# Graph transformer layer: the down projection of the steady slots alternates two graphs and two PSUM banks matmul by matmul

## Chip, cores and metric

One core of one Trainium2 chip. The metric is the device time of one launch in microseconds (us); the median of the runs is compared.

## What is computed

128 graphs of 128 nodes with 384 features go through one transformer layer with a dense bias, and then an outer residual and a layer norm:

```python
scores = einsum(q, k) * dh ** -0.5 + adj[:, None]        # 8 heads of 48
x1 = rmsnorm(x + softmax(scores) @ v @ wo + bo) * alpha1 + gamma1
ff = silu(x1 @ w1 + b1) @ w2 + b2                        # 384 -> 1536 -> 384
y  = rmsnorm(x1 + ff) * alpha2 + gamma2
out = layernorm(x + y)
```

Everything is fp32. Each weight product is made of three passes, since every operand is held as a rounded high part and the rest (`PASSES`: low by high, high by low, high by high).

## The kernel before, in words

All weights stay on chip. The graphs are taken in 64 groups of two (`PAIR`; the two graphs of a group are b=0 and b=1). The program of every engine is a list of 68 slots written out by hand (`run_slots`). In slot t five groups are in work at once, each in another stage: the projections to q, k and v of group t-1 (`g_proj`), attention of t-2 (`g_attn`), the up projection of t-3 (`g_ff1`), the down projection and the last norms of t-4 (`g_ff2`), and the transposition of the input of group t. Slots 4 to 64 run the steady program; slots 2 and 3 (`starting`) and 65 to 67 (`ending`) have orders of their own.

Each engine works through its own list strictly in order, and the engines meet at semaphores only. The orders in a steady slot are:

- TensorE (`@block.tensor`, lines 658 to 687): `scores` of both graphs, `down` b=0 (36 matmuls into the bank `ps_rows0`), `down` b=1 (36 into `ps_rows1`), `project_qk` (54 matmuls in three groups of 18; the third waits for `qk_ready[0]`, line 539), `transpose_probs`, `transpose_x1`, `project_v` b=0, `context` of both, `project_v` b=1 (which waits for `x1T_lo[0]`, line 551), `output_product` of both (each waits for `ctx_lo[b]`, line 491), `transpose_x`, and `up` (108 matmuls).
- VectorE (`@block.vector`, lines 1034 to 1079): `bias_and_max` twice, `normalise` 0, `residual2` 0, `normalise` 1, `norm2_and_stats` 0, `residual2` 1, `layer_norm` 0, `norm2_and_stats` 1, `layer_norm` 1, `keys_out`, the low parts of x1 transposed (`transposed_lo`, which makes `x1T_lo`), `values_out` 0, `context_lo` 0 and 1, `values_out` 1, and so on.
- ScalarE (lines 816 to 847): 16 exponentials, `sum_of_squares` 0 of the second residual (waits for `res2_ready[0]`), a load of the Silu table, `sum_of_squares` 1, `queries_out` 0 and 1.
- GpSimd (lines 413 to 438): the inverse roots of b=0 (RMS, then standard deviation), those of b=1, and after them one addition of 128x768 elements, x1 plus b2 (line 433), which waits only for the transposition of x1.
- SyncE issues the loads, the store of y (it waits for both `layer_norm`s) and after it the ten moves of q and k (line 383).

`residual2` adds x1 to the result in `ps_rows[b]` (line 955), `norm2_and_stats` scales by the inverse RMS (line 960), adds the outer residual (966) and takes the statistics (968, 970), and `layer_norm` is one `tensor_scalar` (line 974). `keys_out` (line 901) empties the third group of `project_qk`.

Of the kernel before, what the change touches and what calls it, by code (L numbers as in the profile page):

```python
# [35 lines left out]
P = 128  # L36
PAIR = 2
# [5 lines left out]
PASSES = ((LO, HI), (HI, LO), (HI, HI))  # L43
# [7 lines left out]
def build_layer(nc, x, adj, wq, bq, wk, bk, wv, bv, wo, bo, w1, b1, w2, b2,  # L51
                alpha1, gamma1, alpha2, gamma2, out):
    graphs, nodes, d = x.shape
# [7 lines left out]
    fc = f // P  # L61
# [6 lines left out]
    with ctx:  # L68
# [221 lines left out]
        def live(g):  # L290

            return 0 <= g < groups

        def through(g, each=1):

            return (g + 1) * each
# [146 lines left out]
        def _(pe):  # L443
# [59 lines left out]
            def down(g, b):  # L503

                last_attn = g + LAG_FF2 - LAG_ATTN - 1
                if live(last_attn):
                    pe.wait_ge(res1_ready[b], through(last_attn))
                elif live(g - 1):
                    pe.wait_ge(res2_ready[b], through(g - 1))
                if b == 0 and live(g + LAG_FF2 - 1):  # L510
                    pe.wait_ge(xT_lo[1], through(g + LAG_FF2 - 1))
                if b == 1:
                    pe.wait_ge(x1T_lo[1], through(g + 1 if ending(g + LAG_FF2) and live(g + 1) else g))
                for m in range(fc):
                    if b == 0 and m % 2 == 0:
                        pe.wait_ge(h_lo[m // 2], through(g))
                    for i, (sta, mov) in enumerate(PASSES):
                        mm = pe.matmul(ps_rows[b][:, 0:d], h[:, sta, m, b * P:(b + 1) * P], w2_s[:, mov, m, :],  # L518
                                       start=(m == 0 and i == 0), stop=(m == fc - 1 and i == len(PASSES) - 1))
                mm.then_inc(down_done[b], 1)  # L520

            def project_qk(g):
                for i in range(2):
                    pe.wait_ge(xT_lo[i], through(g))
                for n, blocks in enumerate((((wq_s, 0), (wq_s, 1)), ((wq_s, 2), (wk_s, 0)),
                                            ((wk_s, 1), (wk_s, 2)))):
                    if g == 0 and n < 2:
                        pe.wait_ge(weight_split, (n + 1) * kd)

                    if n == 0 and live(g - LAG_FF1 + LAG_PROJ - 1):  # L530
                        pe.wait_ge(silu_ready[fc // 2 - 2], through(g - LAG_FF1 + LAG_PROJ - 1))
                    elif n == 0 and live(g - 1):
                        pe.wait_ge(v_ready[1], through(g - 1))
                    elif n == 1 and live(g - LAG_FF1 + LAG_PROJ - 1):
                        pe.wait_ge(silu_ready[fc // 2 - 1], through(g - LAG_FF1 + LAG_PROJ - 1))
                    elif n == 1 and live(g):
                        pe.wait_ge(xT_lo[0], through(g))
                    elif n == 2:
                        pe.wait_ge(qk_ready[0], through(g))
                    for j, (w, c) in enumerate(blocks):  # L540
                        mm = passes(ps_work[n % 2][:, j * toks:(j + 1) * toks], [
                            (lambda part, kb=kb: w[:, part, kb, c * P:(c + 1) * P],
                             lambda part, kb=kb: xT[:, part, kb, :]) for kb in range(kd)])
                    mm.then_inc(qk_done[n], 1)
# [69 lines left out]
            def slot_program(t, parity):  # L614
                g_proj, g_attn, g_ff1, g_ff2 = t - LAG_PROJ, t - LAG_ATTN, t - LAG_FF1, t - LAG_FF2
                if starting(t):
                    for b in range(PAIR):
                        scores(g_attn, b)
                    project_qk(g_proj)
                    for b in range(PAIR):  # L620
                        project_v(g_proj, b)
                    for b in range(PAIR):
                        transpose_probs(g_attn, b)
                    for b in range(PAIR):
                        context(g_attn, b)
                    if live(g_ff1):
                        transpose_x1(g_ff1, parity)
                    if t == LAG_ATTN:
                        pe.wait_ge(weight_split, out_units)
                    for b in range(PAIR):  # L630
                        output_product(g_attn, b)
                    for i in range(2):
                        transpose_x(t, i)
                    if live(g_ff1):
                        pe.wait_ge(weight_split, up_units)
                        up(g_ff1)
                    return
                if ending(t):
                    if live(g_attn):
                        for b in range(PAIR):  # L640
                            scores(g_attn, b)
                    down(g_ff2, 0)
                    if live(g_ff1):
                        transpose_x1(g_ff1, parity)
                    if live(g_attn):
                        transpose_probs(g_attn, 0)
                    down(g_ff2, 1)
                    if live(g_attn):
                        transpose_probs(g_attn, 1)
                    if live(g_ff1):  # L650
                        up(g_ff1)
                    if live(g_attn):
                        for b in range(PAIR):
                            context(g_attn, b)
                        for b in range(PAIR):
                            output_product(g_attn, b)
                    return
                if live(g_attn):
                    for b in range(PAIR):
                        scores(g_attn, b)  # L660
                if live(g_ff2):
                    if t == LAG_FF2:
                        pe.wait_ge(weight_split, len(units))
                    for b in range(PAIR):
                        down(g_ff2, b)
                if live(g_proj):
                    project_qk(g_proj)
                if live(g_attn):
                    for b in range(PAIR):
                        transpose_probs(g_attn, b)  # L670
                if live(g_ff1):
                    transpose_x1(g_ff1, parity)
                if live(g_proj):
                    project_v(g_proj, 0)
                if live(g_attn):
                    for b in range(PAIR):
                        context(g_attn, b)
                if live(g_proj):
                    project_v(g_proj, 1)
                if live(g_attn):  # L680
                    for b in range(PAIR):
                        output_product(g_attn, b)
                if live(t):
                    for i in range(2):
                        transpose_x(t, i)
                if live(g_ff1):
                    up(g_ff1)
# [164 lines left out]
        def _(dve):  # L852
# [26 lines left out]
            def normalise(g, b):  # L879
                for half in range(2):  # L880
                    heads = slice(half * hp, (half + 1) * hp)
                    dve.wait_ge(exp_ready[b], through(g, 2) - 1 + half)
                    dve.reciprocal(row_inv[:, b, heads], row_sum[:, b, heads]).then_inc(inv_ready[b], 1)
                    dve.wait_ge(inv_ready[b], through(g, 2) - 1 + half)
                    dve.tensor_tensor(probs[:, b, heads], probs[:, b, heads],  # L885
                                      row_inv[:, b, heads].unsqueeze(2).to_broadcast([P, hp, P]),
                                      ALU.mult).then_inc(probs_ready[b], 1)
# [89 lines left out]
            def slot_program(t, parity):  # L977
# [56 lines left out]
                if live(g_attn):  # L1034
                    for b in range(PAIR):
                        bias_and_max(g_attn, b, parity)
                    normalise(g_attn, 0)
                if live(g_ff2):
                    residual2(g_ff2, 0, parity)
                if live(g_attn):  # L1040
                    normalise(g_attn, 1)
                if live(g_ff2):
                    norm2_and_stats(g_ff2, 0)
                    residual2(g_ff2, 1, parity)
                    layer_norm(g_ff2, 0)
                    norm2_and_stats(g_ff2, 1)
                    layer_norm(g_ff2, 1)
                if live(g_proj):
                    keys_out(g_proj)
                if live(g_ff1):  # L1050
                    transposed_lo(g_ff1, 0, ps_work[0], x1T_hi, x1T, x1T_lo)
                    transposed_lo(g_ff1, 1, ps_rows[1], x1T_hi, x1T, x1T_lo)
# [53 lines left out]
```

## Time and profile before

| | us |
|---|---|
| median of 3 runs (2967.24 to 2967.73) | 2967.57 |
| the profiled execution | 2968.35 |
| its span in the profile | 2966.6 |
| TensorE busy | 2923.2 (99%) |
| VectorE busy | 1974.3 (67%) |
| ScalarE busy | 1441.6 (49%) |
| GpSimd busy | 697.8 (24%) |

The profile has one row for each group of instructions: its start and its length in us, engine, line, operation, output and inputs, and how many. Where an engine had been idle, the end of the row says for how long and who ended the wait. PE is the matmuls of TensorE and PEld its weight loads, DVE is VectorE, ACT is ScalarE, POOL is GpSimd, and SPq is the queue of SyncE. A steady slot lasts 45.43 us and looks the same every time, so one is read for all.

### The profile page before, as it was taken

Reading aid. Unit: us, or ns where it says so; the run is one execution under the profiler, and the core shown is the slowest. Engines: PE = TensorE matmul, PEld = TensorE weight load, DVE = VectorE, ACT = ScalarE, POOL = GpSimd, SP = SyncE. Lnnn points to the kernel's source line nnn. Section 1 sums busy time; section 2 is a strip of 40 time slices with the busy share of each in tenths; the row PEclk is TensorE's granted clock in tenths of the full one; section 3 lists DMA queues with packets and bytes.
Section 4 is the critical chain, followed back from the end, with each engine's and each line's share of the span. In section 5 each row is a group of like instructions: output and inputs, shape, how many; then the busy total and the mean of one; then the engine's idle time right before and its main releaser. Section 6 shows DMA issues by size and latency. Waiting matters only on the chain.

```text
span 2966.6 us, 62752 instructions
## 1 busy us (share of the span) xinstructions
PE 2923.2 (99%) x25216; PEld 2871.9 (97%) x25216; DVE 1974.3 (67%) x3621; ACT 1441.6 (49%) x4260; POOL 697.8 (24%) x968
## 2 busy tenths in 40 slices
PE   7999999999999999999999999999999999999998
PEld 6999999999999999999999999999999999999998
DVE  5766666666666676666666666666666667666665
ACT  5455455454554454544545545545445445454442
POOL 0222222222222222222222222222222222222222
PEclk9999999999999999999999999999999999999999
DMA  5211211211212112112122121121121211211200
GB/s 163 74 57 47 69 53 50 69 47 56 68 35 69 56 47 69 52 52 69 41 63 59 45 68 54 50 69 48 55 69 36 68 56 47 69 52 51 63 28 28
DMA packets 155491, 171.93 MB, mean 58 GB/s; under 512 B 18624, under 2 KB 155200, under 8 KB 155200
## 3 DMA queue, kind: packets, MB, share of 16 engines
q1 hardware_dynamic: 155200, 167.91, 19.1%
q8 instruction: 200, 3.28, 0.5%
q14 instruction: 91, 0.75, 0.1%
HBM read 92.35 MB, written 25.17 MB: 40 GB/s over the span
## 4 chain that ended last, share of the span: by engine, by line
PE 96%; DVE 1%; ACT 1%; SPq 1%; issue 0%; POOL 0%; DMA 0%; POOLq 0%; ACTq 0%; DVEq 0%
PE ps_work L450 48%; PE ps_rows L518 27%; PE ps_rows L450 6%; PE ps_att L462 4%; PE ps_att L471 4%; PE ps_att L482 2%; PE ps_att L486 2%; PE ps_work L560 2%; PE ps_rows L560 1%; SPq L331 0%; ACT probs L704 0%; DVE w_s L864 0%; SPq L383 0%; ACT squares L719 0%; DVE neg_max L876 0%
## 5 line engine op out<-in xcount | busy, mean ns | idle before, releaser
L450 PE MATMUL ps_work<-x1T,w_s 128*128 128x256 f32 x6912 | 847.7, 283 | 2.9 <-ACT h_raw L760 2.2
L450 PEld LDWEIGHTS ps_work<-x1T,w_s 128*128 128x128 f32 x6912 | 835.6, 188 | 3.5 <-ACT h_raw L760 2.4
L518 PE MATMUL ps_rows<-w_s,h 128*128 128x384 f32 x4608 | 822.2, 339 | 10.7 <-DVE x1T L922 7.0
L518 PEld LDWEIGHTS ps_rows<-w_s,h 128*128 128x128 f32 x4608 | 801.4, 189 | 18.7 <-issue 7.4
L760 ACT ACTIVATE h_raw<-ps_work,b_col 128x256 f32<-128x256 f32 x768 | 322.7, 471 | 478.5 <-PE ps_work L450 471.3
L704 ACT ACTIVATE probs<-probs,neg_max 128x128 f32<-128x128 f32 x1024 | 396.0, 388 | 238.5 <-DVE neg_max L876 238.5
L946 DVE TENSOR_TENSOR h<-h_raw,h 128x512 fp32r<-128x512 f32 x384 | 359.3, 936 | 13.2
L944 DVE CAST h<-h_raw 128x512 fp32r<-128x512 f32 x384 | 165.7, 431 | 302.7 <-ACT h_raw L760 302.2
L419 POOL TENSOR_TENSOR x_last<-x_last,rows 128x768 f32<-128x768 f32 x64 | 117.7, 1839 | 773.8 <-PE ps_att L462 773.8
L407 POOL TENSOR_SCALAR mean_sq<-sum_sq 128x1 f32<-128x1 f32 x256 | 69.0, 270 | 975.4 <-ACT squares L719 975.3
L450 PE MATMUL ps_work<-wv_s,xT 128*128 128x384 f32 x1152 | 235.2, 348 | 2.1 <-ACT qk_flat L740 1.2
L450 PE MATMUL ps_work<-xT,wq_s 128*128 128x256 f32 x1728 | 217.4, 283 | 4.0 <-DVE wq_s L864 2.9
L450 PEld LDWEIGHTS ps_work<-xT,wq_s 128*128 128x128 f32 x1728 | 214.9, 191 | 4.7 <-issue 3.5
L450 PE MATMUL ps_work<-xT,wk_s 128*128 128x256 f32 x1728 | 213.5, 280 | 0.0
L450 PE MATMUL ps_rows<-wo_s,ctxT 128*128 128x384 f32 x1152 | 210.7, 336 | 1.3 <-DVE ctxT L891 1.2
L450 PEld LDWEIGHTS ps_work<-wv_s,xT 128*128 128x128 f32 x1152 | 196.4, 188 | 14.9 <-issue 12.1
L450 PEld LDWEIGHTS ps_work<-xT,wk_s 128*128 128x128 f32 x1728 | 207.5, 188 | 0.3 <-ACT qk_flat L737 0.3
L450 PEld LDWEIGHTS ps_rows<-wo_s,ctxT 128*128 128x128 f32 x1152 | 200.3, 188 | 2.1 <-issue 1.1
L719 ACT ACTIVATE squares<-x 128x384 f32<-128x384 f32 x128 | 67.5, 527 | 272.8 <-DVE x L929 272.6
L704 ACT ACTIVATION_READ_ACCUMULATOR probs<-probs,neg_max 128x1 f32 x1024 | 192.1, 188 | 0.0
L723 ACT ACTIVATE probs<-ps_att 128x1024 f32<-128x1024 f32 x128 | 124.5, 1024 | 131.9 <-PE ps_att L471 131.9
L885 DVE TENSOR_TENSOR probs<-probs,row_inv 128x512 f32<-128x512 f32 x256 | 178.3, 697 | 8.8
(86 smaller groups left out, 3440.7 us busy)
## 6 DMA issues: line engine op xcount, KB each, us to landing
qk<-qk_flat SPq DMA_DIRECT2D x384, 96.0 KB, 2.4
x_in<-in_x SPq DMA_DIRECT2D x64, 384.0 KB, 3.2
x_res<-in_x SPq DMA_DIRECT2D x64, 384.0 KB, 3.9
x_last<-in_x SPq DMA_DIRECT2D x64, 384.0 KB, 3.2
out<-y SPq DMA_DIRECT2D x63, 384.0 KB, 2.5
bias<-in_adj SPq DMA_DIRECT2D x64, 128.0 KB, 3.8
qk<-qk_flat SPq DMA_DIRECT2D x128, 64.0 KB, 2.1
qk<-qk_flat SPq DMA_DIRECT2D x128, 32.0 KB, 2.0
```

Source lines behind the costliest of these rows:

```text
L419: pool.tensor_tensor(x_last[:], x_last[:], row(GAMMA2), ALU.add).then_inc(x_last_biased, 1)
L450: mm = pe.matmul(ps_out, stationary(sta), moving(mov), start=(i == 0), stop=(i == n - 1))
L462: mm = pe.matmul(ps_att[b][:, at:at + P], qk[p0:p0 + dh, Q, c, b * P:(b + 1) * P], qk[p0:p0 + dh, K, c, b * P:(b + 1) * P], start=True, st ...
L471: mm = pe.transpose(ps_att[b][:, head * P:(head + 1) * P], probs[:, b, head, :], ident[:])
L518: mm = pe.matmul(ps_rows[b][:, 0:d], h[:, sta, m, b * P:(b + 1) * P], w2_s[:, mov, m, :], start=(m == 0 and i == 0), stop=(m == fc - 1 and ...
L560: mm = pe.transpose(ps_out[:, at:at + P], rows_in[:, b, kb * P:(kb + 1) * P], ident[:])
L704: e = act.activation(probs[:, b, head, :], probs[:, b, head, :], ACT.Exp, bias=neg_max[:, b, head:head + 1], accum_out=row_sum[:, b, head: ...
L723: act.activation(probs[:, b].rearrange("p h n -> p (h n)"), ps_att[b][:], ACT.Copy).then_inc(probsT_ready[b], 1)
L760: e = act.activation(h_raw[:, m % 2, j * toks:(j + 1) * toks], ps_work[m % 2][:, j * toks:(j + 1) * toks], ACT.Silu, bias=b1_col[:, 2 * m ...
L885: dve.tensor_tensor(probs[:, b, heads], probs[:, b, heads], row_inv[:, b, heads].unsqueeze(2).to_broadcast([P, hp, P]), ALU.mult).then_inc ...
L944: dve.tensor_copy(hi, h_raw[:, m % 2, :]).then_inc(h_hi[m], 1)
L946: dve.tensor_tensor(h[:, LO, 2 * m:2 * m + 2, :].rearrange("p c n -> p (c n)"), h_raw[:, m % 2, :], hi.bitcast(F32), ALU.subtract).then_in ...
```

## The change

A new function `down_alternating` takes the place of the two calls of `down` in the steady slots. It runs the same 72 matmuls, but each pass of each block is done for b=0 and then for b=1, so that successive matmuls go to different banks, and both sums are finished at the end. All its waits stand ahead of or inside the joint loop. On VectorE the steady order is changed too: `normalise` 0 and 1, `residual2` 0 and 1, `norm2_and_stats` 0, `layer_norm` 0, then `keys_out`, and only then `norm2_and_stats` 1 and `layer_norm` 1. ScalarE, GpSimd and SyncE keep their programs, and so do the starting and ending slots.

```diff
--- before.py
+++ after.py
@@ -518,6 +518,27 @@
                         mm = pe.matmul(ps_rows[b][:, 0:d], h[:, sta, m, b * P:(b + 1) * P], w2_s[:, mov, m, :],
                                        start=(m == 0 and i == 0), stop=(m == fc - 1 and i == len(PASSES) - 1))
                 mm.then_inc(down_done[b], 1)
+
+            def down_alternating(g):
+
+                last_attn = g + LAG_FF2 - LAG_ATTN - 1
+                for b in range(PAIR):
+                    if live(last_attn):
+                        pe.wait_ge(res1_ready[b], through(last_attn))
+                    elif live(g - 1):
+                        pe.wait_ge(res2_ready[b], through(g - 1))
+                if live(g + LAG_FF2 - 1):
+                    pe.wait_ge(xT_lo[1], through(g + LAG_FF2 - 1))
+                pe.wait_ge(x1T_lo[1], through(g))
+                for m in range(fc):
+                    if m % 2 == 0:
+                        pe.wait_ge(h_lo[m // 2], through(g))
+                    for i, (sta, mov) in enumerate(PASSES):
+                        for b in range(PAIR):
+                            mm = pe.matmul(ps_rows[b][:, 0:d], h[:, sta, m, b * P:(b + 1) * P], w2_s[:, mov, m, :],
+                                           start=(m == 0 and i == 0), stop=(m == fc - 1 and i == len(PASSES) - 1))
+                            if m == fc - 1 and i == len(PASSES) - 1:
+                                mm.then_inc(down_done[b], 1)
 
             def project_qk(g):
                 for i in range(2):
@@ -661,8 +682,7 @@
                 if live(g_ff2):
                     if t == LAG_FF2:
                         pe.wait_ge(weight_split, len(units))
-                    for b in range(PAIR):
-                        down(g_ff2, b)
+                    down_alternating(g_ff2)
                 if live(g_proj):
                     project_qk(g_proj)
                 if live(g_attn):
@@ -1034,19 +1054,18 @@
                 if live(g_attn):
                     for b in range(PAIR):
                         bias_and_max(g_attn, b, parity)
-                    normalise(g_attn, 0)
+                    for b in range(PAIR):
+                        normalise(g_attn, b)
                 if live(g_ff2):
-                    residual2(g_ff2, 0, parity)
-                if live(g_attn):
-                    normalise(g_attn, 1)
+                    for b in range(PAIR):
+                        residual2(g_ff2, b, parity)
+                    norm2_and_stats(g_ff2, 0)
+                    layer_norm(g_ff2, 0)
+                if live(g_proj):
+                    keys_out(g_proj)
                 if live(g_ff2):
-                    norm2_and_stats(g_ff2, 0)
-                    residual2(g_ff2, 1, parity)
-                    layer_norm(g_ff2, 0)
                     norm2_and_stats(g_ff2, 1)
                     layer_norm(g_ff2, 1)
-                if live(g_proj):
-                    keys_out(g_proj)
                 if live(g_ff1):
                     transposed_lo(g_ff1, 0, ps_work[0], x1T_hi, x1T, x1T_lo)
                     transposed_lo(g_ff1, 1, ps_rows[1], x1T_hi, x1T, x1T_lo)
```

## Rows read from the trace of the kernel before

**Rows 1.** The page's first part: busy time and instructions by engine.

```profile
PE 2923.2 (99%) x25216; PEld 2871.9 (97%) x25216; DVE 1974.3 (67%) x3621; ACT 1441.6 (49%) x4260; POOL 697.8 (24%) x968
```

**Rows 2.** Chain of work, one steady slot: start, length, what.

```profile
1508.08 12.68 PE ps_rows L518 x72
1520.76 6.34 PE ps_work L450 x54
...
1534.76 3.12 PE ps_rows L450 x18
```

**Rows 3.** Chain of work, the ending slots.

```profile
2913.37 6.25 PE ps_rows L518 x36
...
2946.12 12.51 PE ps_rows L518 x72
```

**Rows 4.** Instructions in order of time, one steady slot, from down to keys_out.

```profile
1518.28 0.51 ACT L719 ACTIVATE squares<-y 128x384 f32<-128x384 f32 x1
...
1518.90 1.28 ACT L822 ACT_TABLE_LOAD   x1
...
1521.97 0.53 DVE L955 TENSOR_TENSOR y<-ps_rows,x 128x384 f32<-128x384 f32 x1
...
1522.53 0.53 ACT L719 ACTIVATE squares<-y 128x384 f32<-128x384 f32 x1 [2.35 <-DVE y L955]
...
1523.05 0.82 ACT L737 ACTIVATE qk_flat<-ps_work,bq_col 128x256 f32<-128x256 f32 x2
...
1523.66 3.24 PEld L450 LDWEIGHTS ps_work<-xT,wk_s 128*128 128x128 f32 x27
...
1524.20 0.62 DVE L960 SCALAR_TENSOR_TENSOR y<-y,inv_rms,rows 128x384 f32<-128x384 f32 x1 [0.72 <-POOL inv_rms L410]
...
1527.17 0.48 DVE L974 TENSOR_SCALAR y<-y,mean_var,inv_std 128x384 f32<-128x384 f32 x1 [0.95 <-POOL inv_std L410]
1527.57 0.87 DVE L901 TENSOR_SCALAR qk_flat<-ps_work,bk_col 128x256 f32<-128x256 f32 x2
```

**Rows 5.** The same view and slot, from the moves of q and k on.

```profile
1528.54 7.06 SPq L383 DMA_DIRECT2D qk<-qk_flat  x10
...
1529.65 1.85 POOL L433 TENSOR_TENSOR x<-x,rows 128x768 f32<-128x768 f32 x1 [2.51 <-PE ps_rows L560]
...
1530.48 0.69 DVE L922 TENSOR_TENSOR x1T<-ps_work,x1T 128x512 fp32r<-128x512 f32 x1 [2.04 <-ACT x1T L747]
...
1531.08 0.41 DVE L922 TENSOR_TENSOR x1T<-ps_rows,x1T 128x256 fp32r<-128x256 f32 x1
...
1532.24 0.42 DVE L911 TENSOR_TENSOR v_first<-ps_work,rows 128x256 f32<-128x256 f32 x1 [0.74 <-PE ps_att L486]
...
1532.85 0.55 DVE L891 TENSOR_TENSOR ctxT<-ps_att,ctxT 128x384 fp32r<-128x384 f32 x1
1532.91 1.53 PEld L450 LDWEIGHTS ps_work<-wv_s,xT 128*128 128x128 f32 x9 [0.20 <-issue]
...
1534.43 3.13 PEld L450 LDWEIGHTS ps_rows<-wo_s,ctxT 128*128 128x128 f32 x18
```

**Rows 6.** The same view, ending slots.

```profile
2898.14 0.55 POOL L410 TENSOR_TENSOR inv_std<-var_eps,neg_half 128x1 f32<-128x1 f32 x1
2898.66 1.84 POOL L433 TENSOR_TENSOR x<-x,rows 128x768 f32<-128x768 f32 x1
2898.73 1.99 DVE L974 TENSOR_SCALAR y<-y,mean_var,inv_std 128x384 f32<-128x384 f32 x1 [0.95 <-POOL inv_std L410]
...
2922.08 0.41 DVE L922 TENSOR_TENSOR x1T<-ps_rows,x1T 128x256 fp32r<-128x256 f32 x1
...
2922.61 7.76 PEld L518 LDWEIGHTS ps_rows<-w_s,h 128*128 128x128 f32 x36 [2.58 <-issue]
```

**Rows 7.** Busy time by stretch: stretch, length, engines, granted clock, DMA share, GB/s.

```profile
2922.60:2930.50 7.90, 7.86 (x36) 7.89 (x37) 2.20 (x5) 0.00 (x0) 0.74 (x2) 0.78 0.00 0
```

## Prediction, made before the changed kernel was run

> **What bounds the kernel.** I read the busy times first, then the chain of work through one steady slot, then the instructions of that slot in order of time. TensorE is busy for 99% of the span [rows 1], and in a steady slot the chain is TensorE alone, piece behind piece, such as 12.68 us of down projection, 6.34 of q and k, 3.12 of output product [rows 2]. So a change can help only by making matmuls themselves shorter, and it hurts as soon as one of TensorE's waits ends late. The edit touches 61 slots (t = 4 to 64); 1 us in each would be 61 us.
>
> **The matmuls.** Nothing is removed or added: 72 matmuls and 72 weight loads of the same shapes in each slot. New is that 71 successive pairs change the bank, where one did. The trace has no continuous alternation; it has single changes. The 36 matmuls into one bank take 6.25 us, 173.6 ns each; 72 with one change take 12.51 [rows 3], so a change costs 0 to 0.02 us by rounding. The output product is 18 matmuls of the same width with one change in 3.12 us [rows 2], 173.3 ns each, against 18 x 173.6 = 3.125, so a change costs -12 to +3 ns. Both together leave 0 to 3 ns; over 70 x 61 = 4270 further changes that is 0 to 13 us. I take 0, since the stretch with one change in 18 is no slower per matmul than that with none. TensorE's waits move too: those of b=1 on `res1_ready[1]` and `x1T_lo[1]` go from the middle to the start. Both were signalled in the slot before (the low parts of x1 end at 1531.49 for a down that starts 22 us later [rows 2, 5]), so they cost nothing, and `h_lo` is needed later than before, not earlier.
>
> **The moved end of b=0.** Before, b=0 is done halfway, at about 1514.4, and its second norm is computed while b=1 runs. Now b=0 ends one matmul ahead of b=1, at 1520.76 - 0.17 = 1520.59 on the clock of the slot shown [rows 2]. Everything behind it must fit into the gaps up to TensorE's next waits. I go through them with the durations of [rows 4]; a waiting engine starts 0.03 to 0.04 us after the one it waits for.
>
> ScalarE: residual2 of b=0 runs from 1520.63 to 1521.16. The Square starts at 1521.20, the table load 0.62 later (as 1518.28 to 1518.90) and lasts 1.28, to 1523.10; that load was hidden in the down projection and now stands behind it. The Square of b=1 starts there, and the query copy 0.52 later (as 1522.53 to 1523.05), at 1523.62, and lasts 0.82, to 1524.44. TensorE's third group of q and k needs that bank at the tenth of the 27 loads, 1523.66 + 9 x 0.117 = 1524.71 [rows 4]. It fits, with some 0.2 us left. Cost 0; if the cover is missed by 0.1 us, 6 us in all.
>
> VectorE up to `keys_out`: norm 2 of b=0 starts at most 1.67 us behind its Square (1522.53 to 1524.20), so by 1522.87, and layer_norm 0 follows 2.97 later (1524.20 to 1527.17), 1525.84 to 1526.32. Then `keys_out` waits for the last matmul of q and k, 1520.76 + 6.34 = 1527.10 [rows 2], and runs from 1527.14 to 1528.01; before, it began at 1527.57 [rows 4]. That is 0.43 us earlier, and nobody on the chain gains by it.
>
> VectorE behind `keys_out`: what queues behind that wait is norm 2 of b=1, whose inputs are there by then (GpSimd has its inverse RMS by 1525.8 + 1.67 = 1527.5 at the latest). It starts at 1527.93, since a ready instruction starts some 0.08 before its predecessor's end (1530.48 + 0.69 against 1531.08 [rows 5]). layer_norm 1 is due 2.97 later, at 1530.90, where it was done at 1527.65 [rows 4]: 3.7 us later.
>
> Here it meets GpSimd. The addition of 128x768 elements (line 433) stands in GpSimd's list behind the inverse deviation of b=1. In before it starts at 1529.65, when x1 is transposed [rows 5], and layer_norm 1 is long over. Now it is released by the same event as layer_norm 1. The ending slots hold just this case: the inverse deviation ends at 2898.69, GpSimd's addition starts at 2898.66, layer_norm at 2898.73, and the latter takes 1.99 us and not 0.48; it ends 0.22 behind the addition [rows 4, 6]. So layer_norm 1 waits for the addition. In the new slot: addition 1530.83 to 1532.68, layer_norm 1 until 1532.90.
>
> The Trainium skill (SBUF - State Buffer, Who interferes with whom) has this as an exclusive lock: whichever of VectorE and GpSimd issues first keeps the shared port pair, and the other blocks for the whole instruction; `tensor_scalar` is named among those that can take it. The trace agrees, with 1.99 us against 0.48. By the rule alone the sum would be the same.
>
> What is late next: the low part of x1 (0.69) starts at 1532.81 and ends at 1533.50 instead of 1531.17. `project_v` of b=1 waits for it and started its weights at 1532.91 [rows 5]. From such a low part to the weight load behind it there are 0.12 us (2922.49 to 2922.61 [rows 6]), so it starts at 1533.62. **Stall: 0.71 us.** Then `ctx_lo[0]`: from the first low part to the end of line 891 VectorE needs 0.60 (to 1531.08), 0.33 for the second part, 0.61 (1532.24 to 1532.85) and 0.55 [rows 5], which gives 1534.90, seen by TensorE at 1535.02; the output product is now due at 1534.43 + 0.71 = 1535.14. It fits by 0.1. From there the slot runs as before.
>
> Side effects off the chain: SyncE waits for layer_norm 1, so the ten moves of q and k start near 1533.8 and not 1528.54; with 7.06 us of issue [rows 5] they end at 1541, and `scores` needs them ten us later. The next loads start 2 us later and have more room than that.
>
> **Sum.** 61 x 0.71 = 43 us, with 0 for the matmuls. The profiled execution took 2968.35 (span 2966.6 and 1.75 around it), so 3011.3 by its measure; the median is 0.78 lower, so 3010.6. The stall is a difference of chained starts and may be off by 0.2 us; 0.5 to 0.9 us gives 31 to 55. With up to 13 for the bank changes, 2998 to 3036, and the larger ends of all are unlikely together.
>
> **Rivals.**
> - *layer_norm 1 is not held* (chance 0.13): it gets in ahead of GpSimd, or the addition starts later than I think. Then it ends at 1531.38, the low part at 1531.98, seen at 1532.10, ahead of 1532.91, and no wait of TensorE ends late: 2967.6, no change. It decides at 0.07 us, the lead of the addition over layer_norm in [rows 6]; that the same queue order gave that lead there speaks against it.
> - *Alternation makes matmuls shorter* (0.04): 384 columns at 2.4 GHz are 160 ns of the 173.6. If all of the rest went, 4392 x 13.6 = 60 us would come back against 43 lost, and the time would be 2951. It decides at 9.8 ns a matmul; the stretch with one change in 18 shows 0.3.
> - *ScalarE is late as well* (0.08): the query copy misses 1524.71 by up to 0.3 us, everything behind shifts with it, and up to 18 us come on top: 3012 to 3029.
> - *TensorE's clock falls* (0.02): each slot now has nearly a microsecond without a matmul. In the ending slots the mean granted clock was 0.78 in a stretch [rows 7] behind 2.58 us of idling, so in part at the lower level of 1.2 GHz. Its 36 weight loads took 7.76 us [rows 6] against 6.25 for 36 matmuls at full clock [rows 3], 1.5 lost; 61 such losses are 92: 3102. The Trainium skill (TensorE: Matmul & The Clock Gate, A second HAM failure mode: psum-queue depth-cycling) warns that cycling through banks makes TensorE pause and its clock swing; by that page this rival would be likelier, but the single changes of bank here show no pause.
> - *Another wait is late too* (0.02), such as the 0.1 us at the output product: above 3032.
>
> **How the numbers follow.** The forecast has 0.71. The range 2990 to 3032 holds it with the ScalarE case, 0.79; outside lie no change, the gain and the two dearer cases. What a measurement can tell from no change is 0.2%, 6 us, or 0.1 us of stall in a slot. Slower: 0.71 + 0.08 + 0.02 + 0.02 = 0.83; same 0.13; faster 0.04.
>
> **What would show it.** Right: a layer_norm of about 2 us in every steady slot beside line 433, the steady slot 46.1 us long, and TensorE's idling ahead of `project_v`'s second half put down to x1T, some 0.7 us 61 times. The 72 matmuls of down stay at 12.7 us. Wrong: layer_norm at 0.48 us, a down piece shorter or longer than 12.7, idling ahead of the q and k product, or a granted clock under 1 in the middle of the span.

## The result and the profile after

The changed kernel takes 3012.07 us (median of 4 runs, 3009.1 to 3013.83) against 2967.65 before: a ratio of 1.0148, 95% interval 1.0135 to 1.0162. It is 44.4 us slower; 3010.6 was forecast, in a range of 2990 to 3032. The span of the profiled execution is 3007.3 us, 40.7 more than before, and that execution (3009.1) is the fastest of the four.

TensorE's waits, longest first (who waited for whom: us in total, times, longest), have one line that the kernel before has nothing to answer to:

```profile
PE ps_work L450 <- DVE x1T L942: 39.4, 61, 0.6
```

It is the second `project_v`, 61 times, once in each changed slot. The chain of work (start, length, what) through one slot shows where that wait comes from:

```profile
1528.66 12.68 PE ps_rows L538 x72
1541.34 6.36 PE ps_work L450 x54
...
1547.72 0.88 DVE qk_flat L921 x2
1548.60 0.54 DVE y L980
...
1550.89 0.56 POOL inv_std L410
...
1551.47 1.30 DVE y L994
...
1553.38 0.69 DVE x1T L942
...
1554.20 1.83 PE ps_work L450 x9
1556.03 3.12 PE ps_rows L450 x18
...
1574.78 12.68 PE ps_rows L538 x72
```

The down projection is as long as in [rows 2], 12.68 us; the next one starts 46.12 us after this one, where a slot took 45.43. Between the q and k product and `project_v` the chain leaves TensorE: `keys_out` (L921), the norm of b=1 (L980 to L990), GpSimd's inverse deviation (L410), layer_norm (L994), the low part of x1 (L942). In before this stretch was TensorE alone. (layer_norm's length is split here, 1.30 us and then 0.60 in which the chain finds nothing that it waits for; the rows below have it whole.) The same slot in order of time, in the lines that answer to [rows 4, 5]:

```profile
1541.30 1.02 DVE L975 TENSOR_TENSOR y<-ps_rows,x 128x384 f32<-128x384 f32 x2 [1.41 <-PE ps_rows L538]
1541.89 0.53 ACT L739 ACTIVATE squares<-y 128x384 f32<-128x384 f32 x1 [2.94 <-DVE y L975]
...
1542.53 1.28 ACT L842 ACT_TABLE_LOAD   x1
...
1544.24 3.24 PEld L450 LDWEIGHTS ps_work<-xT,wk_s 128*128 128x128 f32 x27
...
1544.35 0.82 ACT L757 ACTIVATE qk_flat<-ps_work,bq_col 128x256 f32<-128x256 f32 x2
...
1547.72 0.88 DVE L921 TENSOR_SCALAR qk_flat<-ps_work,bk_col 128x256 f32<-128x256 f32 x2 [0.82 <-PE ps_work L450]
1548.51 0.61 DVE L980 SCALAR_TENSOR_TENSOR y<-y,inv_rms,rows 128x384 f32<-128x384 f32 x1
...
1551.41 1.83 POOL L433 TENSOR_TENSOR x<-x,rows 128x768 f32<-128x768 f32 x1
1551.47 1.98 DVE L994 TENSOR_SCALAR y<-y,mean_var,inv_std 128x384 f32<-128x384 f32 x1 [0.95 <-POOL inv_std L410]
...
1553.38 0.68 DVE L942 TENSOR_TENSOR x1T<-ps_work,x1T 128x512 fp32r<-128x512 f32 x1
...
1554.17 1.53 PEld L450 LDWEIGHTS ps_work<-wv_s,xT 128*128 128x128 f32 x9 [0.89 <-issue]
...
1554.90 1.01 DVE L911 TENSOR_TENSOR ctxT<-ps_att,ctxT 128x384 fp32r<-128x384 f32 x2
1555.70 2.44 PEld L450 LDWEIGHTS ps_rows<-wo_s,ctxT 128*128 128x128 f32 x14
```

The two lines to look at are those at 1551.41 and 1551.47: GpSimd's addition of line 433 starts 0.06 us ahead of layer_norm 1, and layer_norm takes 1.98 us instead of 0.48. It does so in all 61 changed slots (1.98 to 1.99 us). The profile gives GpSimd's times only roughly, so the lead of 0.06 us is less certain than the length on VectorE. The low part of x1 (L942), the weight loads of `project_v` and what follows stand in its train.

### The profile page after: what moved, and what is told of

It is laid out like the page before. It is cut to its first block, busy times and chain, and to the rows that moved or that the text cites. A ratio compares the mean times of both kernels' runs of the same rounds, so it can differ in the third digit from the quotient of the medians.

```text
span 3007.3 us, 62752 instructions
## 1 busy us (share of the span) xinstructions
PE 2924.2 (97%) x25216; PEld 2870.6 (95%) x25216; DVE 2055.4 (68%) x3621; ACT 1448.1 (48%) x4260; POOL 675.1 (22%) x968
## 4 chain that ended last, share of the span: by engine, by line
PE 83%; DVE 11%; issue 2%; POOL 2%; ACT 1%; SPq 1%; DMA 0%; POOLq 0%; ACTq 0%; DVEq 0%
PE ps_work L450 44%; PE ps_rows L538 26%; PE ps_rows L450 6%; PE ps_att L462 4%; DVE y L994 3%; DVE qk_flat L921 2%; DVE x1T L942 1%; DVE stats L988 1%; DVE y L986 1%; PE ps_rows L518 1%; POOL inv_std L410 1%; DVE y L980 1%; PE ps_work L581 1%; SPq L331 0%; PE ps_rows L581 0%
## 5 line engine op out<-in xcount | busy, mean ns | idle before, releaser
L538 PE MATMUL ps_rows<-w_s,h 128*128 128x384 f32 x4392 | 779.3, 338 | 3.7 <-DVE w_s L884 3.7
L538 PEld LDWEIGHTS ps_rows<-w_s,h 128*128 128x128 f32 x4392 | 759.7, 188 | 11.2 <-DVE w_s L884 3.9
L407 POOL TENSOR_SCALAR mean_sq<-sum_sq 128x1 f32<-128x1 f32 x256 | 49.7, 194 | 1122.8 <-ACT squares L739 1117.4
L450 PE MATMUL ps_work<-wv_s,xT 128*128 128x384 f32 x1152 | 233.8, 347 | 41.5 <-DVE x1T L942 39.4
L994 DVE TENSOR_SCALAR y<-y,mean_var,inv_std 128x384 f32<-128x384 f32 x128 | 156.2, 1220 | 121.0 <-POOL inv_std L410 121.0
```

What stands on the lines that cost most here:

```text
L450: mm = pe.matmul(ps_out, stationary(sta), moving(mov), start=(i == 0), stop=(i == n - 1))
L994: dve.tensor_scalar(y[:, b, :], y[:, b, :], mean_var[:, b, 0:1], inv_std[:, b:b + 1], ALU.subtract, ALU.mult).then_inc(y_ready[b], 1)
```

## The experiments

The theory: the time is lost where VectorE's order puts layer_norm 1 behind `keys_out`, into GpSimd's addition, with the low part of x1 queued behind it; the alternation itself costs the matmuls nothing. The rivals: alternation costs (matmuls, or the late end of b=0); the later queue costs, collision or none; line 433 and layer_norm slow each other whoever is first. The kernel before was run beside each; its median was 2967.6 to 2967.8.

### Moving keys_out alone

The kernel before, `down` b=0 and then b=1, with one edit:

```diff
                     layer_norm(g_ff2, 0)
-                    norm2_and_stats(g_ff2, 1)
-                    layer_norm(g_ff2, 1)
                 if live(g_proj):
                     keys_out(g_proj)
+                if live(g_ff2):
+                    norm2_and_stats(g_ff2, 1)
+                    layer_norm(g_ff2, 1)
```

> The kernel before with one thing moved: on VectorE keys_out stands ahead of norm2_and_stats 1 and layer_norm 1; TensorE does not alternate. Theory of the held layer_norm: layer_norm 1 starts 2.97 us behind a keys_out that ends at the same place of the slot as in the changed kernel, meets line 433 and takes 1.98 us, project_v of b=1 waits for x1T, slot 46.12 us, time 3007 to 3014. Rival, that the alternation or the late end of b=0 costs the time: about 2968.

Measured: 3011.65 us, ratio 1.0149 (1.0133 to 1.0164). TensorE's waits have the same line as in the changed kernel:

```profile
PE ps_work L450 <- DVE x1T L922: 39.4, 61, 0.6
```

So this one move makes the whole loss, without alternation.

### VectorE's new order without the alternation

The kernel before with VectorE's part of the diff, TensorE's part left out.

> The kernel before with VectorE's whole new order and TensorE's old one (b=0, then b=1). Theory (the loss sits in VectorE's order, whatever TensorE does): layer_norm 1 is held behind keys_out, x1T comes 0.65 us late, slot 46.12 us, 3007 to 3014, the same as the changed kernel, though b=0 is done 6 us earlier and the table load is hidden again. Rival, that alternation and its late b=0 carry part of the 44 us: less than 3000.

Measured: 3010.24 us, ratio 1.0143 (1.0129 to 1.0157), and 39.4 us of the same wait in 61 times. Alternating or not, the time is the same once VectorE's order is the new one.

### The alternation without VectorE's new order

The changed kernel with VectorE's part of the diff left out.

> The changed kernel with VectorE's old order: TensorE alternates, residual2 0 stands ahead of normalise 1 and residual2 1 behind norm2_and_stats 0. Theory (the alternation is free for the matmuls, the late end of b=0 is dear for the queues): the down piece stays 12.68 us; residual2 1 comes at about 4.2 us behind the end of down, ScalarE's queries_out behind its Square is 2.1 us late for the third group of q and k, and keys_out behind layer_norm 1 holds the transposes of x1 for 0.8 us more; slot 48.3 us, time 3130 to 3160. Rival, that only VectorE's new order costs time: 2968.

Measured: 3190.03 us, ratio 1.075 (1.0732 to 1.0768): more than expected. The waits of TensorE are the two foreseen:

```profile
PE ps_work L450 <- ACT qk_flat L757: 137.0, 61, 2.2
PE ps_work L581 <- DVE qk_flat L921: 18.7, 35, 0.5
```

The first is 2.25 us a slot, where 2.1 was expected. In order of time, and then the busy time of two stretches (in the last columns: granted clock, DMA share, GB/s):

```profile
1540.06 0.52 ACT L739 ACTIVATE squares<-y 128x384 f32<-128x384 f32 x1 [2.62 <-DVE y L975]
...
1540.58 1.19 ACT L757 ACTIVATE qk_flat<-ps_work,bq_col 128x256 f32<-128x256 f32 x3
...
1541.45 3.55 PE L450 MATMUL ps_work<-xT,wk_s 128*128 128x256 f32 x18 [2.25 <-ACT qk_flat L757]
```

```profile
1541.45:1545.00 3.55, 3.55 (x19) 3.55 (x20) 2.22 (x5) 0.68 (x2) 0.98 (x3) 0.62 0.28 58
...
1570.00:1600.00 30.00, 27.21 (x254) 26.23 (x253) 18.94 (x34) 15.54 (x49) 9.49 (x11) 1.00 0.14 40
```

The 18 matmuls behind the wait take 3.55 us instead of 2.12 (a third of 6.34 [rows 2]), at a mean granted clock of 0.62: part of them ran at 1.2 GHz. The next stretch holds another such stall (TensorE is busy for 27.21 of its 30 us) and kept its clock, so the clock falls behind some stalls and not behind others. What a fall costs a slot is read from the chain of work, from one down piece to the next (71 of its 72 matmuls are on the chain here):

```profile
1522.29 12.52 PE ps_rows L538 x71
...
1571.81 12.52 PE ps_rows L538 x71
...
1620.49 12.52 PE ps_rows L538 x71
```

The slot with the fallen clock lasts 49.52 us, the one without 48.68. The matmuls lose twice as much as these 0.84 us: in the chain the 18 take 1.43 us more, and the 16 transposes of the probabilities behind them 2.14 us instead of 1.75. But TensorE then comes late to the transposes of x1 and doesn't have to wait for `keys_out`; that wait is there 35 times and not 61. In the whole trace, the first changed slot left aside, 25 slots of 59 have such a fall, and together they are 21 us longer than they would be at the 48.66 us of the slots without one.

The expected slot of 48.3 us gives 2967.8 + 61 x 2.9 = 3145 us, so the expectation misses some 45 us, and less than half of that is the clock. About as much, some 21 us, is the plain slot: it is not 48.3 us, with 0.15 us more in the first stall, and the first four transposes behind the second one take 0.63 us where they take 0.44 without a wait. The rest lies in the first changed slot and in the ending ones.

### keys_out back behind layer_norm 1

The changed kernel with `keys_out` in its old place relative to the norm of b=1, `normalise` and `residual2` in the new one.

> The changed kernel with keys_out back behind layer_norm 1. Theory: with both sums of down ready only at its end, layer_norm 1 starts 9.0 us behind that end and is not held (line 433 waits for transposes that wait for keys_out), 0.48 us; keys_out ends near 10.2 us behind the end of down, where the transposes of x1 were due at 7.8: a stall of 2.5 us, slot 47.9 us, 3120 or, if the clock falls behind such stalls as it did with TensorE alone alternating, up to 3170. Rival, that the place of keys_out is what costs the 44 us in the changed kernel: 2968.

Measured: 3130.15 us, ratio 1.0555 (1.054 to 1.057). In order of time:

```profile
1516.47 0.48 DVE L994 TENSOR_SCALAR y<-y,mean_var,inv_std 128x384 f32<-128x384 f32 x1 [0.95 <-POOL inv_std L410]
1516.86 0.87 DVE L921 TENSOR_SCALAR qk_flat<-ps_work,bk_col 128x256 f32<-128x256 f32 x2
...
1517.85 0.42 PEld L581 LDWEIGHTS ps_work<-ident,x 128*128 128x128 f32 x4 [2.52 <-issue]
```

layer_norm 1 is not held, but the transposes of x1 (L581) wait for `keys_out`: TensorE's loads had been idle for 2.52 us. So with the late b=0 the old place of `keys_out` is dearer than the new one: 163 us against 44. The slot is 47.92 us, as expected, where the clock holds. In the profiled execution, the slowest of the four (3141.14 us), it fell in 12 slots of 59, each about 1.5 us longer, 19 us together; its mean was 0.988.

### The addition in halves

The changed kernel with GpSimd's long instruction cut in two:

```diff
-                    pool.tensor_tensor(x1[:, 1 - parity], x1[:, 1 - parity], row(B2),
-                                       ALU.add).then_inc(x1_b2_ready, 1)
+                    for b in range(PAIR):
+                        e = pool.tensor_tensor(x1[:, 1 - parity, b, :], x1[:, 1 - parity, b, :],
+                                               rows[:, B2, :], ALU.add)
+                        e.then_inc(x1_b2_ready, 1)
```

> The changed kernel with GpSimd's addition of line 433 split in two of 128x384, one for each graph. Theory of the held layer_norm: the first half holds it for some 0.95 us instead of 1.83, layer_norm 1 takes about 1.1 us, x1T_lo comes 0.15 us ahead of project_v, the slot is 45.43 to 45.5 us, time 2968 to 2973. Rival, that the later place of the norm in VectorE's queue costs it by itself: 3010 as before.

Measured: 2968.28 us, ratio 1.0001 (0.9992 to 1.0011).

```profile
1531.27 2.10 POOL L434 TENSOR_TENSOR x<-x,rows 128x384 f32<-128x384 f32 x2
1531.34 1.16 DVE L996 TENSOR_SCALAR y<-y,mean_var,inv_std 128x384 f32<-128x384 f32 x1 [0.95 <-POOL inv_std L410]
```

layer_norm got in between the two halves, 1.16 us, and the x1T wait is gone from the list. The queue is as late as in the changed kernel up to layer_norm's start; only the hold is shorter.

### The addition moved away

The changed kernel with line 433 behind the inverse roots of attention.

> The changed kernel with GpSimd's addition of line 433 moved behind the inverse roots of attention, 10 us later in the slot. Theory of the held layer_norm: layer_norm 1 takes 0.48 us in every slot, x1T is ready 0.8 us ahead of project_v, slot 45.43 us, 2966 to 2972; the addition now meets the first split of h, which has over a microsecond of room. Rival, that the queue behind keys_out is late by itself: 3010, or over 2980 where it is late in part.

Measured: 2967.11 us, ratio 1.0 (0.999 to 1.0009).

```profile
1530.23 0.48 DVE L994 TENSOR_SCALAR y<-y,mean_var,inv_std 128x384 f32<-128x384 f32 x1 [0.94 <-POOL inv_std L410]
...
1530.62 0.69 DVE L942 TENSOR_TENSOR x1T<-ps_work,x1T 128x512 fp32r<-128x512 f32 x1
...
1532.24 1.53 PEld L450 LDWEIGHTS ps_work<-wv_s,xT 128*128 128x128 f32 x9 [0.20 <-issue]
...
1539.52 1.84 POOL L437 TENSOR_TENSOR x<-x,rows 128x768 f32<-128x768 f32 x1
...
1540.94 0.71 DVE L964 CAST h<-h_raw 128x512 fp32r<-128x512 f32 x1 [0.86 <-ACT h_raw L780]
```

layer_norm 1 is 0.48 us; x1T is ready at 1531.31, 0.9 us ahead of the loads of `project_v` at 1532.24. The addition now stretches the first cast of h, 0.71 us against 0.43, and nobody waits.

### The addition issued second

The changed kernel with a tiny instruction ahead of the addition:

```diff
+                    pool.tensor_scalar(idle[:], neg_half[:], 1.0, None, ALU.mult)
                     pool.tensor_tensor(x1[:, 1 - parity], x1[:, 1 - parity], row(B2),
```

> The changed kernel with one tiny GpSimd instruction (128x1, some 0.2 us) put ahead of the addition of line 433, so that layer_norm 1 is issued first. Theory (who comes first holds the other for its whole length): layer_norm 1 takes 0.48 us in the steady slots, the addition ends a little later, by 0.2 to 0.5 us, and is in nobody's way; x1T in time, slot 45.43 us, 2966 to 2970. Rival, that the two slow each other down whenever they overlap, whoever is first: layer_norm 1 over 1 us and a slot over 45.6 us, 2980 or more.

Measured: 2966.53 us, ratio 0.9997 (0.9987 to 1.0006).

```profile
1530.09 0.23 POOL L434 TENSOR_SCALAR idle<-neg_half 128x1 f32<-128x1 f32 x1
1530.15 0.48 DVE L996 TENSOR_SCALAR y<-y,mean_var,inv_std 128x384 f32<-128x384 f32 x1 [0.95 <-POOL inv_std L411]
...
1530.27 2.05 POOL L435 TENSOR_TENSOR x<-x,rows 128x768 f32<-128x768 f32 x1
```

layer_norm starts 0.12 us ahead of the addition and takes its plain 0.48; now the addition is the one that is longer, 2.05 against 1.83. One more instruction of 0.23 us wins back the whole loss (45.5 us from 3012.07). A hold shared by both is ruled out.

The edit also adds a tile of 4 bytes a partition (`idle`), and the times of the matmuls differ a little: the down piece takes 12.83 us in the chain and the up projection 12.87 where it was 12.98, and the slot is 45.40 us. Whether the new tile moved the others is not shown. The hold itself is still there in this kernel: the low part of h (L968) takes 2.20 us instead of 0.69 once in every slot, as its counterpart does in the kernel before. So it is the order that freed layer_norm.

### layer_norm 1 behind the low parts of x1

The changed kernel, with VectorE's `layer_norm(g_ff2, 1)` behind the two `transposed_lo` of x1.

> The changed kernel with layer_norm 1 behind the two transposed_lo of x1 on VectorE. Theory of the held layer_norm: it is held as before, about 1.5 us, but nothing that TensorE needs at once is queued behind it; x1T is ready where it was in the kernel before, ctx_lo[0] some 0.3 us ahead of the output product; slot 45.43 us, 2966 to 2972. Rival, that alternation costs the time: 3010. Rival, that everything behind keys_out is late anyway: x1T waits again, over 2990.

Measured: 2967.66 us, ratio 1.0 (0.9991 to 1.0009).

```profile
1530.25 0.69 DVE L942 TENSOR_TENSOR x1T<-ps_work,x1T 128x512 fp32r<-128x512 f32 x1 [0.53 <-ACT x1T L767]
1530.60 1.84 POOL L433 TENSOR_TENSOR x<-x,rows 128x768 f32<-128x768 f32 x1
...
1530.86 0.41 DVE L942 TENSOR_TENSOR x1T<-ps_rows,x1T 128x256 fp32r<-128x256 f32 x1
...
1531.19 1.46 DVE L994 TENSOR_SCALAR y<-y,mean_var,inv_std 128x384 f32<-128x384 f32 x1
...
1532.68 1.53 PEld L450 LDWEIGHTS ps_work<-wv_s,xT 128*128 128x128 f32 x9 [0.20 <-issue]
```

Here layer_norm is held all the same, 1.46 us, and it costs nothing: what TensorE needs next has already run. The hold is a loss only with the low part of x1 behind it.

### The kernel before with the addition in halves

The same split in the kernel before, for the ending slots, where one held layer_norm lies on the chain.

> The kernel before with the addition of line 433 in two halves. In the steady slots nothing collides, so nothing changes; in the two ending slots layer_norm 1 is held for 1 us less, and one of them has it on the chain: 0 to 1.5 us less in all, 2966 to 2968, which the times can hardly tell. Rival, that a split addition slows GpSimd's queue: up to 61 x 0.25 us more if it were on the chain, 2983.

Measured: 2966.82 us, ratio 0.9998 (0.9989 to 1.0007). The held layer_norm of the ending slots is shorter, here in the chain of work:

```profile
2934.24 1.16 DVE y L976
```

It was 1.98 us. But the cast and the low part of h, next on VectorE, took 2.00 and 0.70 us in the chain before and take 1.17 and 2.21 now: the hold has moved to the next instruction, and 0.14 us of the 0.82 are left. No time beyond the measurement's uncertainty came of it, so neither this nor any other run beats the kernel before by more than its interval.

## Why the prediction came out right

The slot shown above is 20.58 us later on its clock than that of [rows 2] (1541.34 against 1520.76 for the end of down), so every time of the forecast can be laid beside it.

- **The matmuls cost nothing more**: 12.68 us for 72 matmuls with 71 changes of bank. The bounds of 0 to 13 us for the changes were worked out from the ending slots, where 72 matmuls take 12.51 us [rows 3]; like against like is the steady piece, 12.68 [rows 2] and 12.68. That the change would be slower by the alternation itself is refuted from both sides: `keys_out` moved alone makes the same loss without it, and the changed kernel with the addition moved away alternates and loses nothing.
- **ScalarE fits, by less than forecast**: the query copy was to run to 1524.44; it ends at 1545.17, that is 1524.59. The Square of b=0 starts at 1541.89, not 1541.78, since residual2 of b=0 started later than 0.04 us behind its matmul. The loads needed the bank at 1544.24 + 9 x 0.117 = 1545.29, so 0.12 us were left, not 0.27. The rival of a late ScalarE was close.
- **VectorE up to keys_out**: forecast 1527.14, measured 1547.72, that is 1527.14.
- **layer_norm 1 held**: addition and layer_norm forecast for 1530.83 and 1530.90, measured 1530.83 and 1530.89; its end forecast for 1532.90, measured 1532.87. Two rows of the ending slots gave this, and with them the length: 1.99 us there, 1.98 here.
- **The stall**: the weight loads of `project_v` forecast for 1533.62, measured 1533.59. The output product was to fit by 0.1 us, and it does: TensorE's list of waits has no new line for it. A slot of 46.14 us was forecast and 46.12 is measured.
- **The sum**: 61 x 0.69 = 42.1 from the slots, 40.7 in the spans of the two profiled executions, 44.4 between the medians. The forecast of 43 lies between them. The profiled executions have less than 42.1 because the first changed slot grew by 0.30 us only, the next 59 by 0.68 to 0.69. (One slot near the end, the 54th, is 0.34 us longer than the rest in every kernel, the one before too; it cancels.) That the median is 3 us above the profiled execution is not explained; the last point on the hardware below has a candidate.
- **The rivals**: layer_norm first is what the tiny instruction produces, and it gives 2966.53 us where 2967.6 was worked out; the point from which it decides, 0.07 us of lead, was crossed with 0.23 us of other work. The clock did not fall in the changed kernel (mean 0.995 as before), but it did in the two experiments with stalls of 2.3 us.

What the forecast did not say is that the 44 us are the small remainder of a dearer choice. With both sums of down ending together, VectorE's old order costs 222 us and `keys_out` in its old place 163; the new order takes that down to 44, and one instruction in GpSimd's list to 0. Alternation brought nothing to pay with: no matmul got shorter.

## What to carry to other kernels

When a step moves later in an engine's queue, look at what the other engines release by the same event, and read from the trace whether those two instructions have ever overlapped: two rows of an odd slot told 44 us of this one. Where GpSimd's long addition met layer_norm, the one issued first ran at its own length and the other came out longer, so a tiny instruction, a split or another place for the long one was enough. Read from the trace whether your instruction is one that is held, since not every one is (next section). And a held instruction costs only what is queued behind it: put what TensorE needs next ahead of it.

## What the runs showed of the hardware

- A change of PSUM bank from one matmul of 128x384 to the next costs nothing that shows here: 72 of them take 12.68 us with 71 changes (changed kernel) and 12.68 with one (kernel before). With the tiny instruction added, 72 with 71 changes take 12.83; if that were the changes, it would be 2 ns for each.
- A lock between GpSimd and VectorE goes by issue: 0.06 us of lead for GpSimd made layer_norm 1.98 us (changed kernel), 0.12 us of lead for VectorE left it 0.48 and the addition 2.05. The Trainium skill (SBUF - State Buffer, Who interferes with whom) says that issue order decides, and the trace agrees.
- Not every VectorE instruction is held. The two low parts of x1 run inside the addition of line 433 and take their plain 0.69 and 0.41 us [rows 5]; each has one input in PSUM (`ps_work`, `ps_rows`). The low part of h, with both inputs in SBUF, is held once in every steady slot of the kernel before, 2.20 us instead of 0.69, beside another addition of GpSimd:

```profile
1507.28 1.84 POOL L419 TENSOR_TENSOR x_last<-x_last,rows 128x768 f32<-128x768 f32 x1 [12.49 <-PE ps_att L462]
1507.47 2.20 DVE L946 TENSOR_TENSOR h<-h_raw,h 128x512 fp32r<-128x512 f32 x1
```

  TensorE waits for nothing there. So the hold was to be seen in the steady slots too, and not only in the ending ones. No experiment was made on which instructions are held.
- Stalls of 0.65 us in each slot left the clock at its upper level. Stalls of 2.25 us (the alternation alone) let it fall in 25 slots of 59; in the slot shown a fall made the matmuls behind it 1.8 us longer and the slot 0.84. Stalls of 2.31 us (`keys_out` back) let it fall in 12 of 59, at 1.5 us a slot.
- In some slots a stretch ran about 2% slower, with the granted clock at 1.00. In the kernel with `keys_out` moved alone, two successive down pieces in the chain of work, and then the busy time of the second piece and of the first (the granted clock is the third column from the end):

```profile
1483.31 12.68 PE ps_rows L518 x72
...
1529.46 12.91 PE ps_rows L518 x72
```

```profile
1529.46:1542.37 12.91, 12.91 (x75) 12.91 (x75) 11.07 (x16) 8.27 (x36) 4.25 (x4) 1.00 0.00 0
1483.30:1496.00 12.70, 12.70 (x76) 12.70 (x75) 10.87 (x16) 8.28 (x36) 4.25 (x4) 1.00 0.00 1
```

What makes these 0.23 us longer is open: the same instructions, the same clock in the rows, no wait. That trace has six such slots, each 0.30 us longer as a whole, and its execution took 3012.01 us where the changed kernel's profiled one, which has none, took 3009.1. Such slots could be why the runs of each of the three kernels near 3011 us scatter by 1.5 to 4.7 us and why the median of the changed kernel lies above its profiled execution; no profile of the other runs was there to show it.
